# Graph network kernel: dense layers two and three, picked-group selections and edge sums from two float32r parts

## What is computed

```python
def sage_conv(x, src, dst, Wl, bl, Wr, n_nodes):
    summed = jax.ops.segment_sum(x[src], dst, num_segments=n_nodes)
    cnt = jax.ops.segment_sum(ones, dst, num_segments=n_nodes)
    return (summed / jnp.maximum(cnt, 1.0)) @ Wl.T + bl + x @ Wr.T

h = jnp.maximum(_layernorm(x), 0.0)
h = relu(sage_conv(h, src, dst, W1l, b1, W1r, n))
h = relu(sage_conv(h, src, dst, W2l, b2, W2r, n))
x = x + sage_conv(h, src, dst, W3l, b3, W3r, n)

h = jnp.maximum(_layernorm(x), 0.0)
messages = gelu((h[src] + edge_attr) @ We1 + be1) @ We2 + be2
aggregated = jax.ops.segment_sum(messages, dst, num_segments=n)
x = x + gelu(((1.0 + eps) * h + aggregated) @ Wu1 + bu1) @ Wu2 + bu2
```

## Time and profile before

| | us |
|---|---|
| median of 3 runs | 1129.02 (1119.06, 1129.02, 1130.83) |
| the profiled execution | 1121.82 |
| its span, first to last instruction | 1119.4 |
| TensorE busy | 988.1 (88%) |
| VectorE busy | 506.0 (45%) |
| ScalarE busy | 256.2 (23%) |
| GpSimd busy | 375.2 (34%) |

### The profile page before, as it was taken

One profiled execution on the slowest core, in us unless ns is written; L12 is line 12 of the kernel. 1 busy time (PEld: TensorE's weight loads), 2 busy tenths in 40 slices (PEclk: granted clock), 3 DMA queues, 4 the chain that ended last, 5 costly groups with the idle time before them and its releaser, 6 DMA issues.

```text
span 1119.4 us, 16242 instructions
## 1 busy us (share of the span) xinstructions
PE 988.1 (88%) x5619; PEld 604.1 (54%) x5619; DVE 506.0 (45%) x1984; ACT 256.2 (23%) x449; POOL 375.2 (34%) x394
## 2 busy tenths in 40 slices
PE   5879999999999999974967898897899789899896
PEld 2544555554445445541655565564576466556564
DVE  7799999841112111142733343343335244344342
ACT  3666777711011101010111011011011011101111
POOL 1000000000000112165855465645636655665650
PEclk9889999999999999986978899898879989999997
DMA  3200100010000000063332233333233333333330
GB/s 125 51 2 12 12 11 12 12 56 1 1 1 1 10 10 19 10 121 105 100 87 79 81 108 81 97 97 95 82 82 106 82 93 99 83 109 83 92 92 17
DMA packets 47474, 67.60 MB, mean 60 GB/s; under 512 B 15745, under 2 KB 26204, under 8 KB 47260
## 3 DMA queue, kind: packets, MB, share of 16 engines
q1 hardware_dynamic: 35996, 43.16, 14.3%
q0 software_dynamic: 11392, 23.35, 8.1%
HBM read 63.18 MB, written 3.30 MB: 59 GB/s over the span
## 4 chain that ended last, share of the span: by engine, by line
PE 75%; DVE 11%; issue 7%; another core or an unknown queue 4%; ACT 1%; DMA 1%; SPq 0%; ACTq 0%; DVEq 0%
PE f_ps L1193 22%; PE f_ps L1247 22%; PE f_ps L1309 10%; PE f_ps L1233 7%; DVE f_region L616 2%; DVE f_region L614 2%; PE f_ps L1078 2%; DVE f_region L620 1%; DVE f_region L618 1%; PE f_ps L1071 1%; PE f_ps L1168 1%; PE f_ps L1229 1%; PE f_ps L1130 1%; PE f_ps L1255 1%
## 5 line engine op out<-in xcount | busy, mean ns | idle before, releaser
L564 POOL DMA_INDIRECT f_adj<-table,f_table_idx x356 | 353.7, 994 | 251.5 <-DVE f_adj L914 151.9
L1193 PE MATMUL f_ps<-f_adj,f_parts 125*128 125x500 fp8e4 (+1 forms) x1575 | 331.5, 352 | 0.1
L1247 PE MATMUL f_ps<-f_parts 125*128 125x512 bf16 x1125 | 276.4, 396 | 30.5 <-issue 25.5
L1193 PEld LDWEIGHTS f_ps<-f_adj,f_parts 125*128 125x128 bf16 x1575 | 143.5, 97 | 129.9 <-issue 11.1
L1247 PEld LDWEIGHTS f_ps<-f_parts 125*128 125x128 bf16 x1125 | 113.2, 101 | 181.1 <-issue 72.2
L1309 PE MATMUL f_ps<-f_adj 128*128 128x94 f32 (+20 forms) x984 | 141.4, 287 | 42.3 <-issue 32.5
L806 DVE TENSOR_SCALAR f_parts<-f_parts 128x512 bf16<-128x512 f16 x375 | 94.0, 297 | 170.4 <-PE f_ps L1247 93.9
L1309 PEld LDWEIGHTS f_ps<-f_adj 128*128 128x128 f32 x984 | 138.5, 208 | 59.1 <-issue 46.2
L549 POOL TENSOR_TENSOR f_rest<-f_region,f_parts 125x512 f32<-125x512 f32 (+1 forms) x7 | 7.3, 1050 | 462.6 <-ACT f_parts L1033 462.6
L945 ACT CAST f_adj<-f_ps 128x500 f32 x213 | 126.1, 592 | 56.5 <-PE f_ps L1078 40.6
L786 DVE TENSOR_SCALAR f_adj<-f_iota,f_dst_abs 128x94 f32<-128x94 f16 (+4 forms) x416 | 85.6, 273 | 112.4 <-remote 62.8
(11 more groups left out here) (140 smaller groups left out, 532.9 us busy)
## 6 DMA issues: line engine op xcount, KB each, us to landing
f_region<-in_edge_attr_T SPq DMA_DIRECT2D x103, 256.0 KB
f_adj<-table,f_table_idx POOLq DMA_INDIRECT x356
f_parts<-in_src_row SPq DMA_DIRECT2D x15, 256.0 KB
f_adj<-inv SPq DMA_DIRECT2D x1, 1562.5 KB
table<-f_region SPq DMA_DIRECT2D x6, 250.0 KB
out<-f_xT SPq DMA_DIRECT2D x6, 250.0 KB
f_rcntT<-inv SPq DMA_DIRECT2D x5, 250.0 KB, 3.9
f_xT<-in_xT SPq DMA_DIRECT2D x1, 812.5 KB, 5.8
```

Source lines behind the costliest of these rows:

```text
L564: pool.indirect_dma_start(out=rows[:, r % RW, j * D:(j + 1) * D], out_offset=None, in_=table, in_offset=bass.IndirectOffsetOnAxis(ap=table ...
L1193: ins = pe.matmul(ps[:, dense_ps(i):dense_ps(i) + width(c)], parts[0:NP, (l % 2) * 3 + p, b, :], adj[0:NP, b, lo:hi].bitcast(F8), start=b ...
L1247: ins = pe.matmul(z_columns(g), parts[0:NP, 3 + p, b, :], select[0:NP, u % SELECT, :], start=b == 0 and p == 0, stop=b == NB - 1 and p == ...
```

## The change

1. **Dense layers two and three.** The features are split into two parts of type float32r instead of three of bf16 (`pair[1]`, `pair[2]`), by one ACT copy and one DVE subtraction; `mid` and `low` fall away for these layers. The counts are no longer read as fp8: for every unit of a chunk and a block the bytes are converted to float32r in one of five buffers, `wide` (125 x 500, two matmuls use it). Of five conversions DVE does two (L745), ACT two (L1106), POOL one (L621). Columns are made even: 126 for the last chunk. `AFTER` is 8. `mean_rows` multiplies by `UNIT` besides. Layer one stays as it was.
2. **Selections.** The rows are split into two float32r parts (`chosen`), the one-hots are float32r, eight buffers instead of twelve; 25 x 2 matmuls for a picked group. 14 groups are picked instead of 15.
3. **Edge sums.** A message becomes two float32r parts: ACT applies gelu twice (once rounded to float32r, once in float32), DVE subtracts (`message_rest`, L890). The one-hots are float32r, windows have even ends (96 columns for most). Each of the 492 products is two matmuls. They come one turn later, and so do the node updates (`TAKE` to `ADD` each plus one).
4. **Room.** The parts, the selections, `wide` and others share memory; the one-hots of stage one's `nexts` are built in a ring of three; edge features of the first five groups are loaded after the last dense product instead of during stage two; `table_idx` and `group_ends` after the last group of counts; the look for bytes over 15 is seven reductions of one chunk each, two slots apart, and a last one.

```diff
-    PARTS = 3
+    PARTS = (3, 2, 2)
     RATE = 2.3
-    AFTER = 9
+    AFTER = 8
...
-        self.SHARES = 15
+        self.SHARES = 14
...
+        for slot, units in self.units.items():
+            for n, b, i in units:
+                if n >= s.NC and i == 0:
+                    assert slot >= s.GB
+                    self.put("expand", slot - 1, (n, b))
...
-    CALM = GB + 8
+    CALM = [plan.after + 4 + 2 * c for c in range(NC)]
...
+    WIDE, NEXTS = 5, 3
     AHEAD, OH_AHEAD = 2, 2
-    SELECT = 12
+    SELECT = 8
...
-    TAKE, MIX, SUM, UP, ACTIVE, DOWN, ADD, STORE = 1, 2, 3, 3, 3, 4, 5, 9
+    TAKE, MIX, SUM, UP, ACTIVE, DOWN, ADD, STORE = 2, 3, 4, 4, 4, 5, 6, 9
...
+        TURNS = (ON_DVE, ON_ACT, ON_DVE, ON_ACT, ON_POOL)
...
+        def wait_spent(engine, u):
+            if u % NB == NB - 1:
+                engine.wait_ge(dense_done, NC + u // NB + 1)
+            else:
+                engine.wait_ge(spent, u + 1 - u // NB)
...
-            for g in range(EA):
-                sp.dma_start(ea[:, g, 0:s.tiles(g) * P], edge_columns(g)).then_inc(ea_in[g], 16)
             for c in range(NC):
                 b = s.blocks(c)
+                if c == NC - 1:
+                    sp.wait_ge(dense_done, LAYERS * NC)
+                    for g in range(EA):
+                        sp.dma_start(ea[:, g, 0:s.tiles(g) * P], edge_columns(g)).then_inc(ea_in[g], 16)
                 sp.wait_ge(rows_kept, c + 1)
...
+            def widen_dve(u):
+                if u == 0:
+                    dve.wait_ge(summed, GB)
+                    dve.wait_ge(kept, GB)
+                if u >= WIDE:
+                    wait_spent(dve, u - WIDE)
+                dve.tensor_copy(wide_tile(u), bytes_of(u)).then_inc(widened[ON_DVE], 1)
...
+            def message_rest(g):
+                w = s.tiles(g) * D
+                whole = z_group(g) if g in s.picked else pre[:, s.by_rows(g) % PR, 0:w]
+                dve.wait_ge(rounded, g + 1)
+                dve.tensor_tensor(message[:, g % MS, 1, 0:w], whole, message[:, g % MS, 0, 0:w].bitcast(F32),
+                                  ALU.subtract).then_inc(msg_ready, 1)
...
-                        act.activation(msg[:, g % MS, 0:w], pre[:, s.by_rows(g) % PR, 0:w], ACT.Gelu
-                                       ).then_inc(msg_ready, 1)
+                        act.activation(message[:, g % MS, 0, 0:w], summands, ACT.Gelu)
+                        act.activation(summands, summands, ACT.Gelu).then_inc(rounded, 1)
...
+                    u = ordinal(i, b)
+                    if p == 0:
+                        pe.wait_ge(widened[owner(u)], wide_count(u))
+                    ins = pe.matmul(ps[:, dense_ps(i):dense_ps(i) + streamed(c)], pair[l][0:NP, p, b, :], wide_tile(u),
+                                    start=b == 0 and p == 0, stop=b == NB - 1 and p == 1)
+                    if p == 1 and b < NB - 1:
+                        ins.then_inc(spent, 1)
...
-                for p in range(3):
-                    ins = pe.matmul(z_columns(g), parts[0:NP, 3 + p, b, :], select[0:NP, u % SELECT, :],
-                                    start=b == 0 and p == 0, stop=b == NB - 1 and p == 2, skip_group_check=True)
+                for p in range(2):
+                    ins = pe.matmul(z_columns(g), chosen[0:NP, p, b, :], select[0:NP, u % SELECT, :],
+                                    start=b == 0 and p == 0, stop=b == NB - 1 and p == 1, skip_group_check=True)
...
+                        for p in range(2):
+                            ins = pe.matmul(agg_ps(c, lo, hi), message[:, g % MS, p, j * D:(j + 1) * D],
+                                            onehot[:, g % OH, j, at_lo:at_lo + hi - lo],
```

More of the change, by code:

```diff
@@ L179, in turn @@
     def turn(self, slot, k):
-        later = slot + 6 if slot < self.GB else slot
         self.put("turn", slot, k)
@@ L266, in fast_path @@
+        low, o = carve(by_edge, o, (NT,), F32)
+        src_idx, o = carve(by_edge, o, (NT,), I32)
+        next_key, _ = carve(by_edge, o, (NT,), F16)
+        late, o = carve(by_edge, 0, (2, CHUNK), F32)
+        table_idx, _ = carve(by_edge, o, (FT,), I32)
         iota = sb("iota", [P, CHUNK], F16)
         xT, hT, rcntT = sb("xT", [P, N]), sb("hT", [P, N]), sb("rcntT", [P, N])
[L268 removed]
+        PAIR = 2 * NB * D * 4
+        second, third = slab("second", PAIR), slab("third", PAIR)
```

259 lines of the change are left out of this document (167 added, 92 removed).

## The result

| | before | changed |
|---|---|---|
| median, us | 1129.92 (1119.06 to 1131.53, 4 runs) | 1080.53 (1068.5 to 1083.78, 4 runs) |
| profiled execution, us | 1121.82 | 1083.78 |
| span, us | 1119.4 | 1081.2 |
| granted clock of TensorE, mean | 0.931 | 0.857 |

The ratio is 0.956, 95% interval 0.947 to 0.966: faster by 49 us, where 137 were forecast (1129 to 992). The interval of the forecast held it, its sum did not.

The account below looks back on a forecast made before the run. TensorE was taken to bound the dense layers and the edge stage, GpSimd next. The sum was 1121.8 - 63.3 + 2.5 + 14 - 3 + 5 - 91.8 + 4 + 3 = 992 us, range 940 to 1107.

Parts of the forecast that it names:

- Dense layers two and three: Dense matmuls of 500 columns: 300 fewer at 0.211 us each, a gain of 63.3 us.
- Widening, +14: Converting counts to float32r in the dense layers: rate hidden behind TensorE, order partly exposed, 14 us lost.
- The passage, +5: Passage from dense layers to edges: edge features queued before table rows cost 5 us, between 0 and 12.
- Selections, 0.216 each: Edge stage: 425 fewer selection matmuls at 0.216 us each, a gain of 91.8 us.
- Sums, 0.112: Edge sums: 984 instructions as before, at 0.112 us instead of 0.108, 4 us lost.
- that rival (0.22): Small float32r matmuls cost a whole float32 product: +105 us for sums, +10 for dense, 1107 us; chance 0.22.
- The 156.8 us of other time: Edge stage beyond TensorE's 470.6 us of work: half clock, waits, "issue" stretches; left unchanged in the sum.
- GpSimd is next in line but not the bound: Edge stage: GpSimd's gathers allow no less than about 475 us, the sum puts the stage at 542.6.
- The price of a gather: GpSimd in the edge stage: a gather starts each 1.25 us, 360 take 450 us.
- The clock: Edge stage rival: TensorE idles more, granted clock 0.78 throughout, +60 us, 1052 us; chance 0.06.
- The other time shrinks with the work: Edge stage rival: other time falls 32 us with fewer instructions; with conversions all hidden 946 us; chance 0.14.
- Slower: Dense and selection matmuls rival: float32r takes 0.42 us for 500 columns, +276 us, 1268 us; chance 0.10.

Follow-up runs that it names:

- Q: Condition of the sets of runs in which the kernel before took 980 us, each time steadily; no profile row names what differs.
- D: Condition of the sets of runs in which the kernel before took 1115 to 1130 us; both kernels were first measured in it.
- b_quarter2: Kernel before with only one gather of the four of each group issued, in condition D: 980.2 us, 0.866 of before.
- b_sub: Kernel before with one added VectorE subtraction of 512 columns a turn that nobody waits for, in condition Q: 980.9 us, 0.999 of before.
- b_ring3: Kernel before with three buffers of gathered rows in place of six, in condition Q: 982.9 us, 1.0025 of before.
- b_onepart: Kernel before with two of the three parts of the selected rows left out (375 matmuls instead of 1125), in condition Q: 961.2 us, 0.979 of before.
- a_again: Changed kernel unchanged, measured again beside the kernel before in condition Q: 946.95 us, 0.967 of before.
- a_nosub: Changed kernel with VectorE's message subtraction (L890) cut from 512 columns to two, in condition Q: 937.6 us, 0.955 of before.
- a_quarter2: Changed kernel with only one gather of the four of each group issued, in condition D: 871.8 us, 0.771 of before.
- a_onepart: Changed kernel with the second part of the selected rows left out (350 matmuls instead of 700), in condition Q: 955.7 us, 0.972 of before.

## Why the prediction was wrong, step by step

- **Dense layers two and three: size off, cancelled.** A float32r matmul of 500 columns costs 0.225 us, not the 0.211 of a bf16 one: 600 x 0.014 = 8 us of the 63.3 missing. The small ones cost 0.108 to 0.112, about as taken. The rival of a float32r matmul at 0.42 was far off.
- **Widening, +14:** 1.6 us. The units in hand were enough; this more than gave back what the matmul price took, which is luck. The passage, +5: last dense product to first selection is 18 us instead of 14, right. TensorE's first edge product now waits for edge features and GpSimd 7.1 us for the table. In sum 44.8 us forecast, 47 measured.
- **Selections, 0.216 each:** 0.228 to 0.233. 700 x 0.014 = 10 us less gain. **Sums, 0.112:** 0.104 to 0.112, right; a part does not cost a whole float32 product, and that rival (0.22) falls.
- **VectorE's prices** were right: a selection one-hot of four bytes 438 ns (0.43 taken), a conversion 423 (0.43), a subtraction 677 (0.69).
- **TensorE's side as a whole was right.** Where the gathers are out of the way the change brings 115.5 us (Q) or 108.4 us (D, 980.2 - 871.8); my sum said 129.8 against the profiled execution, and the two prices (18 us) are of the size of what is missing (14 and 21).
- **The step that failed** is "The 156.8 us of other time I leave as they are: the change doesn't touch them by name", together with "GpSimd is next in line but not the bound". b_quarter2 shows that 141 of the 156.8 us go with the gathers (profiled executions, 1121.8 - 980.3; by the medians 149). They were not a block beside TensorE's work that stays when that work shrinks. They were GpSimd's own 604 us from first gather to last, in which TensorE's work was already hidden in part: GpSimd worked 452.6 of those, and waited 151.9 for adds. In condition Q, with the same ring of six, it waits 0.6 us (b_sub), and 24 with a ring of three (b_ring3). The 151.9 us are not work that VectorE has to do: by the order of time the engines that make the adds had been stopped while it gathered. b_onepart shows that even in the quiet condition this kernel had 20 us to gain in the edge stage before GpSimd bounds it, not 92.
- **The price of a gather** was taken as 1.25 us, from two rows with nothing beside them. By the group it was (353.7 + 98.9) / 356 = 1.27, and in the changed kernel (398.7 + 104.7) / 360 = 1.40. 360 x 1.40 from 439.9 on is 943, and 40 us of end make 984: the forecast of 992 had left GpSimd 8 us of waits. I expected 60 of them and did not add them to its row. Written out, the forecast's own row of GpSimd was 441.8 (486.6 less the 44.8 of the dense terms) + 450 of gathers + 60 of waits + 29.3 of end = 981, just under the 992; measured were 439.9 + 503.4 + 97.5 + 40.4 = 1081. Of the 45 us by which the gathers themselves grew (353.7 to 398.7, 4 of them for four more gathers), 23 stand in condition Q too (351.6 in b_ring3 to 375.0 in a_again). Some 8 of these are VectorE's subtraction by a_nosub; the wider one-hots are the likely rest, not shown alone; what adds the other half in D stays open. I had asked only whether VectorE has the time, not whom it stands in the way of.
- **Signs named in advance.** L1320 at 0.21: 0.225. Dense layers in 178 us: 182. GpSimd's wait near 60: 97.5 in D, 0.6 in Q, "near 0 it is the bound" as the prediction said.
- **The clock** fell to 0.78 in the edge stage, as that rival had it. But it fell behind the waits: a_quarter2, in the same condition, has 0.97 there. In a_onepart, in condition Q and with less work for TensorE, it is 0.78 in the edge stage as well, and GpSimd's row alone fills that span (437.4 + 387.8 + 108.5 + 0.9 + 21.8 = 956.4 of 956.5). **The other time shrinks with the work** (946): it did not. **Slower:** no.

## What to carry to other kernels

Before a saving is booked on the busiest engine, write the next engine's ledger from its first to its last instruction (work, gaps, waits, and the end behind it), with the mean of all its instructions and not of two clean ones; what it still waits, and how much earlier it can start, is all that the saving can bring, and it is less if those waits have another cause. Idle time labelled "issue" on several engines at once is not a constant: ask what goes on beside it, and remove that in a run. When work moves to VectorE, price what it does to GpSimd's gathers too. And measure the kernel before again beside every variant: this one took 1129 and 980 us with nothing changed.

## What the hardware showed that I had not expected

- Gathers issued by GpSimd cost the kernel before 149 us in one condition (1129.1 with all, 980.2 with a quarter) and nothing in the other (980.6 and 980.5); in the first, VectorE and ScalarE of the changed kernel get no instruction for up to 16 and 24 us at a time, and TensorE single ones 1.4 us apart. A ring of two buffers in place of six did not cure it (1066.7 us). The cause is open.
- A float32r matmul costs 7% more than a bf16 one at 500 columns (0.225 to 0.211 us), and about half of each of the two instructions of a float32 product (0.42). At 94 to 128 columns one float32r matmul and one float32 instruction both take about 0.11, so there two float32r parts cost as much as one float32 product.
- 71.4 us of VectorE's subtractions in SBUF lengthened 356 gathers by 12.5 us (988 to 1023 ns each), with nothing waiting for them. Gathers started right behind VectorE's adds took 1047 ns in the kernel before and 1792 in the changed one (a quarter of them each).
- Taking 79 us of work from TensorE where it was not the bound left it busy only 28 us less, at a mean clock of 0.866 instead of 0.919.
